# Three phases of a transformer chain on one core: one block of engine programs instead of three, and a new order of products in two steps

## The reference, cut to what matters

```python
# layer 0 (three steps of it are MLPs with gates)
norm = where(m, layernorm(x) * (1 + scale) + shift, 0)
x = x + gate_msa * where(m, mlp(norm, ssm_w1, ssm_w2) + flip(mlp(flip(norm), bwd_w1, bwd_w2)), 0)
x = x + gate_mlp * (gelu_tanh((layernorm(x) * (1 + scale_mlp) + shift_mlp) @ ff_w1 + ff_b1) @ ff_w2 + ff_b2)
# layer 1
xn = (layernorm(x) * ln1_w + ln1_b) * (1 + scale_a) + shift_a
q, k, v = xn @ wq + bq, xn @ wk + bk, xn @ wv + bv        # 16 heads of 32
x = x + softmax(q k^T / sqrt(32)) v @ wo + bo
xn = (layernorm(x) * ln2_w + ln2_b) * (1 + scale_f) + shift_f
x = x + gelu(xn @ w1 + b1) @ w2 + b2                      # 512 -> 2048 -> 512
```

## Time and profile before

| | us |
|---|---|
| median of 3 runs | 1982.2 (1979.6 to 1991.01) |
| profiled execution | 1981.45 |
| its span, first to last instruction | 1979.7 |
| mean granted TensorE clock | 0.988 |

### The profile page before, as it was taken

How to read it: one execution, slowest core, us unless ns; L and a number is a source line. 1 busy time by engine, 2 the same in 40 slices (tenths; PEclk the granted TensorE clock), 3 DMA queues, 4 the chain that set the end, 5 groups by cost and what they waited for, 6 DMA issues and landing times. The chain is left out here.

```text
span 1979.7 us, 33228 instructions
## 1 busy us (share of the span) xinstructions
PE 1915.4 (97%) x11346; PEld 1587.4 (80%) x11346; DVE 1183.8 (60%) x2022; ACT 714.8 (36%) x2104; POOL 488.4 (25%) x579
## 2 busy tenths in 40 slices
PE   5999999999999998999999999799999999999999
PEld 4778888887888887898888897578888888888887
DVE  5577777767777764777777777455252534435222
ACT  3222333332222333777777777331121212122111
POOL 4333333322222221333443443211010101002000
PEclk8999999999999999999999999899999999999999
DMA  8545444444454431666666667522020211102000
GB/s 287 201 157 167 154 152 150 149 141 154 155 179 150 158 133 58 202 212 202 214 203 215 196 215 220 174 72 75 11 86 3 83 43 42 59 25 79 5 22 22
DMA packets 202256, 258.57 MB, mean 131 GB/s; under 512 B 14124, under 2 KB 126344, under 8 KB 202184
## 3 DMA queue, kind: packets, MB, share of 16 engines
q1 hardware_dynamic: 187864, 214.33, 32.4%
q0 software_dynamic: 12160, 39.14, 7.1%
q10 hardware_dynamic: 2160, 4.20, 0.6%
HBM read 166.38 MB, written 91.23 MB: 130 GB/s over the span
## 5 line engine op out<-in xcount | busy, mean ns | idle before, releaser
L614 PE MATMUL banks<-xn,weights 128*128 128x512 f32 x3048 | 734.7, 391 | 5.6 <-DVE xn L879 5.6
L614 PEld LDWEIGHTS banks<-xn,weights 128*128 128x128 f32 x3048 | 574.1, 188 | 130.7 <-DVE xn L879 6.0
L637 PE MATMUL ffn_y<-weights,ffn_h 128*128 128x512 f32 x1536 | 379.5, 397 | 9.9 <-DVE ffn_h L891 9.9
L637 PE MATMUL mlp_y<-weights,mlp_h 128*128 128x512 f32 x1536 | 379.3, 397 | 6.2 <-DVE mlp_h L891 6.2
L637 PEld LDWEIGHTS ffn_y<-weights,ffn_h 128*128 128x128 f32 x1536 | 289.4, 189 | 80.7 <-DVE ffn_h L891 12.0
L637 PEld LDWEIGHTS mlp_y<-weights,mlp_h 128*128 128x128 f32 x1536 | 289.7, 189 | 77.1 <-DVE mlp_h L891 6.7
L766 ACT ACTIVATE ffn_g<-banks,vecs 128x512 f32<-128x512 f32 x128 | 88.2, 689 | 545.5 <-PE banks L614 541.0
L889 DVE CAST ffn_h<-ffn_g 128x512 fp32r<-128x512 f32 x128 | 57.5, 449 | 374.7 <-ACT ffn_g L766 373.8
L766 ACT ACTIVATE mlp_g<-banks,vecs 128x512 f32<-128x512 f32 x128 | 88.0, 688 | 399.6 <-PE banks L614 394.7
L1340 PE MATMUL banks<-xn,weights 128*128 128x256 f32 (+1 forms) x1524 | 193.3, 288 | 5.7 <-DVE xn L1645 5.2
L1340 PE MATMUL banks<-weights,xn 128*128 128x512 f32 x780 | 190.0, 400 | 6.4 <-DVE xn L1678 6.4
(11 more groups left out here) (137 smaller groups left out, 1818.2 us busy)
## 6 DMA issues: line engine op xcount, KB each, us to landing
turned_probs<-att_probs SPq DMA_DIRECT2D x64, 512.0 KB, 3.5
x_tiles<-x SPq DMA_DIRECT2D x98, 256.0 KB, 3.5
x<-x_tiles SPq DMA_DIRECT2D x96, 256.0 KB, 3.4
mlp_bias<-gate_bias_rows POOLq DMA_DIRECT2D x64, 256.0 KB, 4.0
probsT_room<-turned_probs SPq DMA_DIRECT2D x64, 256.0 KB, 4.2
x_tiles<-turned_probs SPq DMA_DIRECT2D x64, 256.0 KB, 3.8
turned_squares<-mlp_xhat SPq DMA_DIRECT2D x62, 256.0 KB, 3.1
mlp_xmod<-turned_squares SPq DMA_DIRECT2D x62, 256.0 KB, 2.9
```

The source lines that it names most:

```text
L614: last = nc.tensor.matmul(m1_bank(c), st.tiles[0](a, k, c), xn[:, parity, b, k, :], start=s == 0, stop=s == len(steps) - 1)
L637: last = nc.tensor.matmul(y_ps[:, tile, :], h[:, c % 2, a, tile * P:(tile + 1) * P], st.tiles[1](b, c), start=c == 0 and s == 0, stop=c == ...
```

## The change

- One `nc.Block` is opened before the first phase and serves all three; `end_phase` is gone. Each engine goes from the last instruction of one phase straight to the first of the next.
- The work buffers that each phase had allocated for itself are now places in shared buffers (`rows`, `h`, `wide`, `spare`, `probs`).
- What the barrier had guaranteed is now waited for one by one: `keys_done` and `chunks_done` for the products done ahead, `y_read`, `pieces_split`, `turned_read`, and the `stored` semaphores. `loads_open` is gone: `load_x` of pair 1 waits until the last block of `mlp` has normalised the tile that lay in the same place, and for the store of the rows it reads.
- The semaphores of `mlp` are cleared by POOL at pair 4 of attention (`clear_first_phase`), and `ffn`, which uses them anew, waits for `cleared`.
- The gate row of the very last tile of `mlp` is loaded into `xhat[:, 0]` after the last squares are stored, not behind the first finished tile.
- In `ffn`, SP loads block 1's x tiles ahead of block 0's, and no longer waits for the landing of block 0's.
- ACT has a one-column Exp at the end of `mlp` and a one-column Gelu ahead of the last `out_high` of `att`.
- In pairs 0 and 1, `values(n, 0)` stands ahead of `scores(n, 0)` on PE. The split of the value bias on DVE moves from the start of `att` to pair 0, ahead of the first maxima.

```diff
-    def end_phase(self, nc):
-        nc.clear_and_free_semaphores(self.semaphores)
-        nc.all_engine_barrier()
-        self.semaphores = []
+    def take_semaphores(self):
+        taken, self.semaphores = self.semaphores, []
+        return taken
...
-        block = local.enter_context(nc.Block())
+        block = sh.block
...   # ffn, SP first()
+                    sp.wait_ge(sh.cleared, 1)
                     for q in range(STAGE_RING):
                         load_own_piece(q)
                     for tile in range(TPP):
                         sp.wait_ge(sh.stored["att"][tile], 16 * NPAIR)
+                        load_x(stages[0], 1, 1, tile)
+                    for tile in range(TPP):
+                        load_x(stages[0], 1, 1, TPP + tile)
                     for tile in range(TPB):
                         load_x(stages[0], 0, 0, tile)
...   # SP, block 0
-                    for tile in range(TPB):
-                        sp.wait_ge(x_loaded[tile], 16)
-                        load_x(after, 1, 1, tile)
+                    if room:
+                        for tile in range(TPB):
+                            sp.wait_ge(x_loaded[tile], 16)
+                            load_x(after, 1, 1, tile)
...
+            def load_final_gate():
+                row = sh.gates_dram[stages[-1].gate].rearrange("(n t) d -> n (t d)", t=TPB)[NBLK - 1:NBLK, GATE_RING * D:]
+                sp.wait_ge(squares_stored, 16 * (swaps(total, TPP - 1) + 1))
+                sp.dma_start(xhat[:, 0, :], row.to_broadcast([P, D])).then_inc(gate_loaded, 16)
...   # ACT, end of mlp
+            if following:
+                nc.scalar.activation(sh.unused[:, 0:1], sh.neg_half[:, 0:1], ACT.Exp).then_inc(passed_act, 1)
...   # att, POOL
                 if n == 1:
-                    pool.wait_ge(loads_open, 1)
+                    pool.wait_ge(sh.turned_read[0], sh.turned_read[1] + tile + 1)
+                    pool.wait_ge(sh.stored["mlp"][TPP + tile], 16 * (NBLK + 1))
...
+            def clear_first_phase():
+                pool.wait_ge(stored[0], 16)
+                pool.wait_ge(xn_ready, tiles_before(CLEARED_AT - 1, 1) + 1)
+                nc.clear_and_free_semaphores(sh.first_semaphores)
+                pool.sem_inc(sh.cleared, 1)
...   # att, PE pair_step(n)
                 if is_pair(n - 2):
                     project(n - 2, 1)
+                elif is_pair(n):
+                    values(n, 0)
                 if is_pair(n):
                     scores(n, 0)
                 if is_pair(n - 1):
                     weigh(n - 1, 0)
-                if is_pair(n):
+                if is_pair(n - 2) and is_pair(n):
                     values(n, 0)
+                if is_pair(n):
                     values(n, 1)
...   # att, ACT last_steps
                 piece_high(NPAIR - 1)
+                nc.scalar.activation(sh.unused[:, 0:1], sh.neg_half[:, 0:1], ACT.Gelu).then_inc(passed_act, 1)
                 out_high(NPAIR - 1, 1)
...   # att, DVE pair_step(n)
+                if is_first(n):
+                    split_value_bias()
                 if is_pair(n):
                     row_max(n, 0, 0)
...   # main
+        sh.block = ctx.enter_context(nc.Block())
         mlp_phase(nc, sh, "mlp", [ssm_stage, ff_stage], chunks=HID // P, room=room, t=t)
-        sh.end_phase(nc)
+        sh.first_semaphores = sh.take_semaphores()
```

More of the change, by code:

```diff
@@ L156 @@
 GATE_RING = TPB - 1
+AT_GATE = 3
 NSQ = P // SQ
@@ L761, in activate @@
             def activate(st, n, c):
-                if not (isinstance(n, int) and n == 0 and c < ahead):
+                if isinstance(n, int) and n == 0 and c < ahead:
+                    act.wait_ge(sh.chunks_done, c + 1)
+                else:
                     act.wait_ge(m1_done, chunks * n + c + 1 - ahead)
@@ L905, in finish @@
                     return
-                gate = gate_bc[:, tile % GATE_RING, :]
+                gate = xhat[:, 0, :] if isinstance(n, int) and n == total - 1 and tile == TPB - 1 else gate_bc[:, tile % GATE_RING, :]
                 if st.masked:
@@ L1521, in copy_values @@
                 act.wait_ge(v_done, TPP * n + tile + 1)
-                if not is_first(n):
+                if is_first(n):
+                    act.wait_ge(sh.stored["mlp"][TPP + tile], 16 * 2 * NBLK)
+                else:
                     act.wait_ge(out_done, TPP * (n - 1) + tile + 1)
```

92 lines of the change are left out of this document (62 added, 30 removed).

## The result

The changed kernel takes 1976.76 us in the median of 20 runs (1970.0 to 1983.33), the kernel before, timed beside it on the same chips, 1988.53 us in the median of 20 (1978.39 to 1992.23). The ratio is 0.9946 [0.9935, 0.9957]. That is 11.8 us less, where 12.2 us were forecast; but the forecast time of 1969.3 us was counted down from one profiled execution of 1981.45 us, and the kernel before takes 7 us more than that in the median. The time ended 0.8 us outside the range.

A forecast was written before the change was run, and what follows sets the result against it. PE, busy 97% of the span, bounds the kernel; only its idle time and slow clock at the two hand-overs can be won. Gains 7.4 + 4.8 = 12.2 us off 1981.45 give 1969.3 us, range 1964 to 1976.

The forecast's parts named there:

- The median may stand some 1.5 us off the profiled run.: Whole kernel: allowance for the measured median differing from the profiled execution, some 1.5 us.
- First hand-over up to the scores: From the first phase's end to attention's first scores: no barrier, earlier x loads, PE without a gap; gain 6.6 us.
- Gain in pair 0: nothing: Attention's pair 0: value products ahead of scores fill one PE wait, but 2.8 us more waiting appears later; gain 0.
- Pair 1: Attention's pair 1: value products moved ahead let exponentials end sooner, limited by the turned probabilities; gain 0.8 us, 0.3 to 1.9.
- Second hand-over: Attention to last phase: block 1's first x tile asked for earlier shortens DVE's wait; gain 4.8 us, 2.5 to 6.6.
- I take 0.6 us off: 1270.7: Second hand-over: `x(1, 0)` lands at 1270.7 instead of 1271.3, since the bias row sharing the queues comes earlier.
- later than 10, the second sum is wrong: Sign at the second hand-over: DVE's x wait should end about 8 us after the first piece, between 6.5 and 10.
- Rival 2: Second hand-over bound by transfers, x tile at 1273 or later, pair 1 waits for probabilities: gain 8.9, 1972.6 us; chance 0.20.
- PE's start at half clock: Second hand-over: if the clock falls, the first 12 matmuls take 4.85 us instead of 2.8, costing nearly nothing.
- Rival 1: Value products gain 2.6 us in each of the first two pairs: total gain 16.6, 1964.9 us; chance 0.08.
- Rival 3: Waits replacing the barriers hold loads back as before; only block-end idle gaps go: 1978.4 us; chance 0.07.
- Rival 4: Slower: Exp table loaded again in each of the pair loop's 12 turns, 15.4 us: 1984.7 us; chance 0.04.

The follow-up runs named there:

- The second profile: The kernel before, unchanged, profiled once more in one run: 1989.75 us.
- The filled kernels: Value bias product done twice on PE ahead of pair 0's second scores: changed kernel 1968.99 us (0.9911); kernel before, also with new product order, 1981.00 us (0.9958).
- the old order: Changed kernel with tile 0's value products put back behind the scores in pairs 0 and 1: 1972.59 us, ratio 0.9928.
- the new order in pair 1 alone: Changed kernel with tile 0's value products put back behind the scores in pair 0 only: 1974.89 us, ratio 0.9937.
- both kernels of the second hand-over: The changed kernel (1976.76 us) and the same with block 1's x tiles counted on semaphores of their own (1972.80 us, ratio 0.9916).

## Why the prediction was wrong in its time, though its sum came out

That 12.2 us forecast and 11.8 us measured in the medians agree is luck. Between the two profiled executions, which the forecast was about, the spans differ by 8.7 us, 3.5 less than forecast: the hole in pair 0 cost 2.56 us that were put at nothing, the second hand-over gave 2.6 us less, and the rest gave 1.6 us more (0.87 of it the earlier A). The medians are further apart than the profiles because the kernel before takes 7.1 us more in its median than in its profile, and the changed kernel 3.9 us more. If the medians lost what the profile lost, the time would have been inside the range without either of the two losses (an estimate: 1976.76 - 2.56 = 1974.2).

- **The base.** The first step that failed is "The median may stand some 1.5 us off the profiled run." It stands 7.1 us off; 12.2 us less than the true median would have been 1976.3. The median of the three runs and the profile agreed within 1 us, but 1991.01 us stood among the three, and the profile showed a clock that stayed full behind two holes of 2.6 us. The second profile lost 7.56 us from A to S2, most of it there, and by their times most executions (48 of 65) look like that one. Against the first group, 1982.4 us, the changed kernel's median is 5.7 us less, against the second, 1989.9, 13.1 us.
- **First hand-over up to the scores: right.** 6.89 us against 6.6. The five products left take 7.36 us against 7.35, without a gap; the first scores start at 772.44, 0.87 us of which is the earlier A; POOL's loads are issued at 746.06; the Exp table is loaded at 753.06 under ACT's idle time.
- **Pair 0: right in the place, wrong in the price.** The scores of tile 0 and tile 1 lie 9.95 us apart before and 9.96 after: the hole only moved. "PE stays busy and keeps its full clock" holds up to the turn; for what follows, the step that failed is "Gain in pair 0: nothing", which priced the hole by its length alone. Its price was -2.56 us in the profile. The filled kernels show it as clock. The kernel before paid it in its second profile, at two holes instead of one, and by their times in most executions; so it is a loss against the first profile, and likely a gain in the medians.
- **Pair 1: right, and worth more where the clock falls.** From the end of its keys to S2 it is 32.45 us before (78.38 - 45.93) and 31.21 after (72.82 - 41.61), so 1.24 us against 0.8. The limit is the one named, the turned probabilities: `weigh` waits 0.97 us for them. Unforeseen was that with this move no hole of over 2 us is left in pair 1, and no profile with it shows slow scores there: 4.15 us between the old order and the new order in pair 1 alone.
- **Second hand-over: 2.2 instead of 4.8 us.** The step that failed is "I take 0.6 us off: 1270.7", or rather what stands behind it, that DVE waits for `x(1, 0)` and nothing else. The landing itself was right: 8.1 us after the first piece were put, 8.25 were measured where only this tile is counted, and C to the end is then 4.8 us shorter, the predicted figure. DVE's wait line is unchanged and so not in the diff; its meaning changed with the order of the loads. The diff does raise POOL's wait on the same semaphores in block 0 from 16 to 32, which could have told it. The mark set ("later than 10, the second sum is wrong") was hit, with 10.85 us. Rival 2 had the right effect for a wrong reason.
- **PE's start at half clock** cost nothing, as said: 12 matmuls in 4.50 us, and the third second product waits 3.02 us for DVE.
- **Rivals.** Rival 1 falls: the hole is in the trace. Rival 3 falls with the loads at 746.06. Rival 4 falls: five table loads before and five after, none in the loop. The clearing on POOL is not to be seen: S2 to C is 422.01 and 421.94 us. But this stretch reaches 424.1 us in other profiles, so a cost under 1 us isn't ruled out.
- **The bounds.** The sum of the first hand-over was given up to 9.4 us; its own parts (6.6 + 1.9, and 0.5 for the chain) give 9.0. No result hangs on it.

## What to carry to other kernels

Price a hole on PE twice: by its length, and by the clock that may fall behind it; where it can't be removed, work of the same length in it, even redundant, was 2.6 us faster here (A to S2). When loads are reordered, read every wait on their semaphores anew and ask which loads its number counts, not which one it was written for. And before a sum is made against one profiled execution, look whether the runs fall into groups and to which of them it belongs.

## What the runs showed of the hardware

- Behind a hole of 2.60 to 2.76 us the granted clock falls in some executions (0.50 in the window from 785 to 790 us of the changed kernel) and stays at 1.00 in others of the same program. In the profiles of this study it stayed behind two such holes, those of the first profile of the kernel before, and fell behind the 13 others in attention's first pairs, at a price of 1.2 to 3.2 us each (from 13.01 against 11.78 us of keys to the 3.19 us behind the second hole of the second profile). What decides it is open. That the same kernel is slow for a different number of matmuls from run to run is what the Trainium skill says of the start of a kernel (TensorE: Matmul & The Clock Gate, section What's actually happening); here it is seen in the middle of one, with 14.34, 13.01 and 13.43 us for the same 96 matmuls.
- The same eight loads of 256 KB were in flight in both kernels of the second hand-over: the first asked for ended DVE's wait 6.3 us after its issue (1261.10 to 1267.4), the fifth 6.6 us after its own (1260.34 to 1266.94). So the queue's later loads didn't hold the first one back, and which load is waited for decided the time.
- The end of attention varies in the same way, in a place that the change doesn't touch. Windows of the 70 us that end at C and the row of the last turn, first for the changed kernel's first profile, then for its second:

```profile
1181.99:1251.99 70.00, 57.20 (x542) 47.58 (x542) 43.46 (x67) 42.78 (x169) 27.34 (x31) 0.93 0.65 204
...
1231.40 0.66 PE L1430 MATMUL wide<-ident,x_tiles 128*128 128x128 f32 x4 [1.90 <-DVE x_tiles L1681]
```

```profile
1183.12:1253.12 70.00, 58.55 (x535) 48.56 (x535) 43.19 (x66) 41.28 (x159) 26.00 (x29) 0.85 0.64 199
...
1233.07 1.11 PE L1430 MATMUL wide<-ident,x_tiles 128*128 128x128 f32 x4 [1.90 <-DVE x_tiles L1681]
```

  PE waits there for DVE again and again, the clock is 0.85 in the second against 0.93, and the same four matmuls take 1.11 instead of 0.66 us behind the same wait of 1.90 us. S2 to C is 423.52 against 421.94 us, and over all profiles it lies between 421.2 and 424.1. Filling those waits was not tried.
